# A second key block weighed in fp32, and the engines' steps in another order, in the fourth stage of a hybrid network

## The reference, cut to what matters

```python
def _L3_attn_ref(x, Wq, bq, Wk, bk, Wv, bv):
    TEMP = (2 * 64) ** 0.5
    q = jnp.einsum('bnf,of->bno', x, Wq) + bq
    k = jnp.einsum('bnf,of->bno', x, Wk) + bk
    v = jnp.einsum('bnf,of->bno', x, Wv) + bv
    scores = jnp.einsum('bnf,bmf->bnm', q, k) / TEMP
    alpha = jax.nn.softmax(scores, axis=-1)
    out = jnp.einsum('bnm,bmf->bnf', alpha, v)
    return out
...
t = t + _L3_attn_ref(_ln_t(t), ...)      # t: (32, 1024, 64), float32
```

## Time and profile before

| | us |
|---|---|
| median of 3 runs | 2915.42 |
| lowest and highest | 2914.91, 2921.2 |
| the profiled execution's own time | 2915.67 |
| its span, first to last instruction | 2913.9 |
| TensorE busy in the span | 2318.3 |
| DVE busy | 2210.4 |
| ACT busy | 2045.3 |
| GpSimd busy | 1645.1 |

### The profile page before, as it was taken

One profiled execution on the slowest core, in us unless ns is written; L12 is line 12 of the kernel. 1 busy time (PEld: TensorE's weight loads), 2 busy tenths in 40 slices (PEclk: granted clock), 3 DMA queues, 4 the chain that ended last, 5 costly groups with the idle time before them and its releaser, 6 DMA issues. The chain is left out here.

```text
span 2913.9 us, 84659 instructions
## 1 busy us (share of the span) xinstructions
PE 2318.3 (80%) x32732; PEld 1731.1 (59%) x32732; DVE 2210.4 (76%) x3688; ACT 2045.3 (70%) x3520; POOL 1645.1 (56%) x1370
## 2 busy tenths in 40 slices
PE   3777777777776699999934565899999999677777
PEld 1555555555554477677723464688888888544444
DVE  4677877777775688898866604788888888688886
ACT  2677777777774699999922201788888888677776
POOL 3577777777775322222166500799999998633331
PEclk9999999999998799999966656899999999799998
DMA  3211111111110000000000020000000000000001
GB/s 72 53 41 37 40 43 37 37 41 36 28 26 1 16 18 14 18 18 18 16 1 1 0 59 0 9 7 7 6 6 7 6 7 6 7 23 22 22 22 26
DMA packets 144658, 62.05 MB, mean 21 GB/s; under 512 B 118676, under 2 KB 127798, under 8 KB 144566
## 3 DMA queue, kind: packets, MB, share of 16 engines
q1 hardware_dynamic: 139565, 58.00, 9.3%
q10 hardware_dynamic: 4393, 2.77, 0.5%
q0 software_dynamic: 608, 0.01, 0.0%
HBM read 14.50 MB, written 8.39 MB: 8 GB/s over the span
## 5 line engine op out<-in xcount | busy, mean ns | idle before, releaser
L1854 POOL TENSOR_TENSOR a_prl<-a_pr,a_prh 128x896 f16<-128x896 f32 x256 | 494.6, 1948 | 54.5 <-ACT a_prh L1836 54.5
L1781 DVE TENSOR_REDUCE a_nmax<-a_ps_a 128x1 f16<-128x1024 f32 x256 | 313.2, 1224 | 58.3 <-PE a_ps_a L1885 56.5
L1198 DVE TENSOR_TENSOR a_exl<-a_ex,a_exh 128x1024 f16<-128x1024 f32 x224 | 275.8, 1260 | 30.1 <-ACT a_exh L1238 29.0
L1832 ACT ACTIVATE a_pr<-a_ps_s 128x1024 f32<-128x1024 f32 x256 | 261.9, 1024 | 32.5 <-PE a_ps_s L1900 20.3
L1898 PE MATMUL a_ps_s<-a_qx,a_kh 128*128 128x128 f16 x2048 | 252.6, 219 | 1.4 <-ACT a_pr L1832 1.1
L1900 PE MATMUL a_ps_s<-a_qm,a_kl 128*128 128x128 f16 x2048 | 252.6, 219 | 0.0
L1233 ACT ACTIVATE a_ex<-a_ps_s,a_shift 128x1024 f32<-128x1024 f32 x224 | 243.1, 1100 | 1.0 <-PE a_ps_s L1281 1.0
L2145 ACT ACTIVATE f_mixed_s<-f_ps_e,f_gates 128x64 f32<-128x64 f32 x1024 | 213.3, 426 | 41.5 <-PE f_ps_e L397 38.6
L1836 ACT ACTIVATE a_prh<-a_pr 128x896 f16<-128x896 f32 x256 | 235.9, 948 | 0.2
L114 POOL TENSOR_TENSOR a_w_hl<-a_xn,a_w_hl 128x512 f16<-128x512 f32 x32 | 36.0, 1125 | 318.7 <-ACT a_w_hl L106 318.7
L1280 PE MATMUL a_ps_s<-a_w_xT 128*128 128x512 f16 x512 | 196.9, 385 | 22.0 <-ACT a_ex L1233 12.3
(11 more groups left out here) (355 smaller groups left out, 8681.7 us busy)
## 6 DMA issues: line engine op xcount, KB each, us to landing
tokens<-in_x_dram SPq DMA_DIRECT2D x32, 256.0 KB, 2.9
bl_qg<-bl_qk_high SPq DMA_DIRECT2D x128, 64.0 KB, 2.0
bl_km<-bl_qk_high SPq DMA_DIRECT2D x256, 32.0 KB, 2.0
a_xTb<-a_w_xT SPq DMA_DIRECT2D x64, 128.0 KB
out_dram<-tokens SPq DMA_DIRECT2D x32, 256.0 KB, 2.6
bl_qg<-bl_qk_low SPq DMA_DIRECT2D x64, 64.0 KB, 2.0
bl_km<-bl_qk_low SPq DMA_DIRECT2D x128, 32.0 KB, 2.0
a_qm<-a_qx SPq DMA_DIRECT2D x64, 64.0 KB, 2.0
```

Source lines behind the costliest of these rows:

```text
L1198: nc.vector.tensor_tensor(exl[:, at[2]], exps(at), exh[:, at[2]], ALU.subtract).then_inc(low, 1)
L1781: nc.vector.tensor_reduce(nmax[:, g:g + 1], ps_a[:], AX.X, ALU.max, negate=True).then_inc(maxed, 1)
L1832: nc.scalar.activation(pr[:, g % RING], ps_s[:, g % 2], ACT.Exp).then_inc(exped, 1)
L1854: nc.gpsimd.tensor_tensor(prl[:, r], pr[:, r, 0:P * SPLIT], prh[:, r], ALU.subtract).then_inc(low, 1)
```

## The change

SPLIT goes from NT - 1 = 7 to NT - 2 = 6. By that, prh and prl hold 768 columns instead of 896, vf two blocks of 65 columns, vh and vl six blocks are used, and a weigh consists of two fp32 matmuls and 18 f16 ones instead of one and 21. The five tables of steps are written anew; the steps in them are the same ones. Of these tables the diff shows two lines; what stands on the engines is below.

```diff
-    SPLIT = NT - 1
+    SPLIT = NT - 2
...
-        DVE_STEPS = [("norm", 0), ("norm", 1), ("range", 3), ("proj", 0), ("norm", 2), ("range", 4),
+        DVE_STEPS = [("norm", 0), ("norm", 1), ("range", 3), ("proj", 0), ("final_last", 2), ("norm", 2),
...
-        SP_STEPS = [("row", 3), ("row", 4), ("row", 5), ("row", 6), ("row", 7), ("copy", 0), ("copy", 1),
+        SP_STEPS = [("copy", 0), ("row", 3), ("row", 4), ("row", 5), ("copy", 1), ("row", 6), ("row", 7),
```

More of the change, by code:

```diff
@@ L1690, in half_of @@
             return slice(512 * (k % 2), 512 * (k % 2) + 512)
[L1692 to L1695, removed]
+        PE_STEPS = [("score", 0), ("range", 3), ("proj", 0), ("weigh_last", 5), ("score", 1), ("range", 4),
+                    ("proj", 1), ("weigh_last", 6), ("weigh_last", 7), ("range", 5), ("score", 2), ("proj", 2),
+                    ("score", 3), ("range", 6), ("weigh", 0), ("weigh", 1), ("range", 7), ("proj", 3), ("score", 4),
+                    ("score", 5), ("range_next", 0), ("score", 6), ("proj", 4), ("range_next", 1), ("weigh", 2),
@@ L1696, in stage_attend_qkv @@
                     ("weigh", 3), ("range_next", 2), ("score", 7), ("norm", 5), ("weigh", 4)]
-        DVE_STEPS = [("norm", 0), ("norm", 1), ("range", 3), ("proj", 0), ("norm", 2), ("range", 4),
-                     ("final_last", 2), ("proj", 1), ("range", 5), ("final_last", 3), ("range", 6), ("proj", 2),
-                     ("range", 7), ("proj", 3), ("final", 0), ("range_next", 0), ("range_next", 1), ("proj", 4),
+        DVE_STEPS = [("norm", 0), ("norm", 1), ("range", 3), ("proj", 0), ("final_last", 2), ("norm", 2),
+                     ("range", 4), ("final_last", 3), ("proj", 1), ("range", 5), ("proj", 2), ("range", 6),
+                     ("final", 0), ("range", 7), ("proj", 3), ("range_next", 0), ("range_next", 1), ("proj", 4),
@@ L1700, in stage_attend_qkv @@
                      ("final", 1), ("range_next", 2), ("norm", 5)]
[L1701 to L1705, removed]
+        ACT_STEPS = [("score", 0), ("proj", 0), ("norm", 1), ("cut", 0), ("score", 1), ("proj", 1), ("cut", 1),
+                     ("proj", 2), ("score", 2), ("score", 3), ("cut", 2), ("cut", 3), ("proj", 3), ("norm", 4),
+                     ("score", 4), ("cut", 4), ("score", 5), ("cut", 5), ("proj", 4), ("score", 6), ("cut", 6),
+                     ("score", 7), ("cut", 7)]
@@ L1706, in stage_attend_qkv @@
+        POOL_STEPS = [("cut", 0), ("cut", 1), ("norm", 2), ("norm", 3), ("cut", 2), ("norm", 4), ("cut", 3),
                       ("cut", 4), ("cut", 5), ("cut", 6), ("cut", 7)]
-        SP_STEPS = [("row", 3), ("row", 4), ("row", 5), ("row", 6), ("row", 7), ("copy", 0), ("copy", 1),
+        SP_STEPS = [("copy", 0), ("row", 3), ("row", 4), ("row", 5), ("copy", 1), ("row", 6), ("row", 7),
                     ("row_next", 0), ("row_next", 1), ("row_next", 2)]
```

## The result

The changed kernel takes 2951.73 us (median of 3 runs, 2951.66 to 2952.26) against 2915.42 before: ratio 1.0119, 95% interval 1.0096 to 1.0142, 36.3 us slower. The forecast was 2941 in a range of 2921 to 2962, so the direction and the range held and the growth, 25.6 us, was 30% too small.

What follows compares the result with a forecast made beforehand. TensorE was taken as the bound, 20.16 us of bare work in a 20.98 us round. Added work 1.00 less 0.11 of stalls gives 0.89; 31 rounds make 27.6, less 2, so 2915.4 + 25.6 = 2941 us, range 2921 to 2962.

Steps and rivals of the forecast that it cites:

- Price of a block: Fourth stage, TensorE: one added fp32 matmul 0.216 us, less three f16 matmuls at 0.091, net +0.125 a tile, +1.00 a round.
- The sign of being wrong: TensorE's weigh: the prediction is wrong if two fp32 blocks take less than 0.40 us from start to start.
- New stall at projection 2: TensorE waits for projection 1's low part, behind final_last 3 on DVE: 1.72 us against 1.32 of work, stall 0.40.
- range_next 0: TensorE waits there for projection 3's low part on DVE: 2.86 us against 2.64 of work, stall 0.22.
- The old stalls at range 5 and weigh_last 6: TensorE: the 0.12 us ahead of range 5 and the old stall at weigh_last 6 both disappear under the new orders.
- the sum of stalls after: TensorE, per round: stalls of 0.71 us after the change against 0.82 before, so a round grows by 0.89.
- range_next 1: TensorE: it comes 1.91 us after the range before it, against 1.82 of work; stall 0.09 in place of 0.37.
- the stage's end: Last image, where TensorE waits for a_prl behind seven cuts: shorter cuts and a sooner tile 6 cut save 2 us.
- B: Rival: the new orders leave TensorE no stall, +4 us, 2919 us; chance 0.10.
- E: Rival: GpSimd's 92% paces the stage, so 2.1 us a round come back, 2850 us; chance 0.02.
- C: Rival: second fp32 block cheap, weight loads hidden under the first's columns; at 0.108 us, 2914 or 2892 us; chance 0.09.
- D: Rival: late ACT copies at projections 2 and 3, stalls 1.6 to 2.5 us, 2969 to 2997 at full size; chance 0.17.

Runs made afterwards that it cites:

- e11: Hand-placed step tables with SPLIT 7, GpSimd made to wait for the centring (L74) ahead of cut 1, not cut 2 as in its predecessor; 2897.4 us, 0.9931 of the kernel before.
- e12: Hand-placed step tables with SPLIT 6, GpSimd made to wait for the centring (L74) ahead of cut 1, not cut 2 as in its predecessor; 2918.8 us, 1.0013 of the kernel before.
- e2: Against the changed kernel, SPLIT put back to 7, so the new orders alone; 2927.4 us, ratio 1.0043 to the kernel before.
- e5: Against the changed kernel, the first fp32 matmul of each weigh issued twice; 3006.9 us, ratio 1.0322 to the kernel before.
- e3: Against the changed kernel, projection 1's low part moved ahead of final_last 3 on DVE; 2937.1 us, ratio 1.0079 to the kernel before.
- e7: Against the changed kernel, SPLIT 7 and all five step tables placed from measured latencies; 2923.2 us, ratio 1.0015 to the kernel before.

## Why the prediction was right, point by point

- **TensorE is the bound, and its work decides: shown.** The block alone cost 23.0 us, relieving GpSimd gave nothing, and doubling the block cost its full 55.2.
- **Price of a block 0.216, net 0.125 a tile, 1.00 a round: held for the change.** After, 22.20 us less the counted stalls (0.45 + 0.21 + 0.21, and 0.28 in every other round, 1.01 a round) leaves 21.19, which is 20.16 + 1.03. For a third block 0.216 was measured directly. The twins of e11 and e12 give 0.095, for the reasons above. The sign of being wrong, two blocks in less than 0.40 us, came true as worded: behind a range they take 0.39. It was set from a single block of 0.23, read behind a score; behind a range the single one takes 0.17, so the added block still costs 0.22.
- **New stall at projection 2, 0.40: right** (0.45), and its cause shown by moving one step (14.7 us back). **range_next 0, 0.22: right** (0.21). **The old stalls at range 5 and weigh_last 6 go:** right but for 0.12 in every other round.
- **The step that was mis-sized is the sum of stalls after, 0.71.** It measured 1.01, and 31 x 0.30 = 9.3 of the missing 10.7 us. Within it, range_next 1 was put at 0.09 by "range start to maximum 0.63", while behind range_next 0 DVE's maximum begins 0.75 us after the range (2206.02). Why is open. It is not the wait ahead of the range as such: the waiting range at 2207.19 of the earlier trace rows and range_next 1 itself have 0.64, and some ranges that did not wait have 0.74. The 0.16 at score 0 and the 0.12 at weigh_last 6 had no row before, and I had counted the places as slack. The rest is small: work of 1.03 for 1.00, and 1 us gained at the stage's end for 2; the first two rounds took 0.9 back.
- **Rivals.** B (no stall left) is out by the 1.01 us of stalls after and by e2, E (GpSimd paces) by e1, C, which needed a block under 0.105 us, by e5. D's stalls of 1.6 to 2.5 us did not come. ACT waits longer for projections (69.4 us in 500 at L1816), but the one stall ahead of a projection went when a step of DVE moved (e3). The share put outside the range, about 0.2, is too small: B, C and E alone are 0.21, without D at full size.
- **Not in the prediction at all:** the exclusion of L74 and GpSimd. It did not change this result, by luck of 0.15 us: in the changed kernel L74 always started first. The forecast of 1.69 us a cut held with the lengthened cuts in both means; the others went from 1.89 to 1.65. In e2 L74 took 0.97 instead of 0.69; whether that is part of that run's 1 us above its range was not tried.

## What to carry to other kernels

On an engine that is 98% busy by its row, add up the distances between starts first: here that gave 20.16 us of bare work in 20.98, and a change that adds 1.0 to it cannot win by relieving an engine nobody waits for. Then walk the order's late spots one by one with latencies measured from start to start, and read each in several places: range start to maximum was 0.63 in some and 0.75 in others. When a part is taken out to price it, look for what becomes late behind it, and price by adding instead. When a stall costs more than the wait itself, look at the granted clock of that stretch.

## What the runs showed of the hardware

- A vector instruction with two SBUF inputs (L74) and a GpSimd tensor_tensor exclude each other: whichever starts second does its work, or nearly all of it, after the first has ended. L74 grew from 0.69 to 2.08 and 2.45 us, to 0.54 after the end of the subtraction of 1.65 or 1.88 us; started first, it lengthened the subtraction from 1.65 to 2.05. With one SBUF input (L85) nothing of the kind was seen. The order flipped on differences under 0.1 us, and a semaphore wait that fixed it gave 2897.4 us where 2923.2 stood, part of it from the clock.
- An fp32 matmul of 128x65 takes 0.216 us of TensorE when it stands among its kind, in two records of 0.108. Alone among f16 matmuls it takes 0.17 to 0.27 us, by what stands ahead; each further one adds 0.22 (0.17, 0.39, 0.61 behind a range).
- After TensorE had stood still for 1.4 us and then 0.5, its granted clock fell to 0.50 (1.2 GHz) for 3.4 us (read in one round); 5 of 13 such rounds of e7 took 1.6 us longer than the others, and the other 8 did not.
